# Feed-forward of a decoder layer on one core: silu and product each as one operation over two banks, and the next tile's XT ahead of the product

## What is computed

```python
def _quant_act(x):
    s = jnp.max(jnp.abs(x), axis=-1, keepdims=True) / 127.0 + EPS
    xq = jnp.clip(jnp.round(x / s), -128.0, 127.0)
    return (xq, s)

def _qlinear(x, w):
    wq, ws = _quant_weight(w)
    xq, xs = _quant_act(x)
    y = jnp.einsum('bsi,oi->bso', xq, wq)
    return y * xs * ws
gate = jax.nn.silu(_qlinear(x, w_gate))
up = _qlinear(x, w_up)
return _qlinear(gate * up, w_down)
...
x = _layernorm(x + _L0_ffn_ref(x, L0_ffn_w_gate, L0_ffn_w_up, L0_ffn_w_down), axis=-1)
```

## Time and profile before

| | us |
|---|---|
| median of 3 runs | 390.02 |
| lowest and highest of the 3 | 386.76, 394.39 |
| span of the profiled execution, first to last instruction | 388.1 |

### The profile page before, as it was taken

How to read it: one execution, slowest core, us unless ns; L and a number is a source line. 1 busy time by engine, 2 the same in 40 slices (tenths; PEclk the granted TensorE clock), 3 DMA queues, 4 the chain that set the end, 5 groups by cost and what they waited for, 6 DMA issues and landing times.

```text
span 388.1 us, 9850 instructions
## 1 busy us (share of the span) xinstructions
PE 276.8 (71%) x3140; PEld 176.7 (46%) x3140; DVE 287.3 (74%) x643; ACT 236.9 (61%) x485; POOL 219.2 (56%) x531
## 2 busy tenths in 40 slices
PE   0262652757757258688999999999897666989862
PEld 0131432535545135455566555555564333555441
DVE  4945899997894344477888888888754349999982
ACT  4349254515676033276777677777737428899993
POOL 5301255564687684566888877888501114576773
PEclk9986588869999657699999999999859669999998
DMA  7992000000000131345333435343300000010111
GB/s 198 329 294 47 0 3 0 0 1 0 0 3 0 27 63 28 63 51 77 64 64 65 64 71 83 70 85 66 58 2 3 0 2 0 14 43 27 41 42 54
DMA packets 53042, 20.38 MB, mean 53 GB/s; under 512 B 42256, under 2 KB 52240, under 8 KB 53008
## 3 DMA queue, kind: packets, MB, share of 16 engines
q1 hardware_dynamic: 53008, 19.95, 23.4%
HBM read 9.32 MB, written 2.10 MB: 29 GB/s over the span
## 4 chain that ended last, share of the span: by engine, by line
PE 26%; DVE 13%; POOL 11%; issue 10%; ACT 4%; DMA 2%; SPq 2%; DVEq 1%; POOLq 0%; ACTq 0%
PE psum L1090 7%; DVE M L943 5%; PE psum L1074 4%; PE psum L1048 4%; PE psum L1032 3%; PE psum L1392 3%; PE psum L1124 3%; ACT PB L864 2%; SPq L709 2%; DVE region_q L1367 2%; DMA region_t<-MT 1%; PE psum L1114 1%; DMA kt<-KA 1%; DVE fxabs L1417 1%; DVE KA L919 1%
## 5 line engine op out<-in xcount | busy, mean ns | idle before, releaser
L943 DVE TENSOR_REDUCE M<-psum 128x8 f32<-128x1024 f32 x64 | 77.6, 1213 | 24.4 <-PE psum L1048 24.1
L864 ACT ACTIVATE PB<-psum,exp_scale 128x1024 f32<-128x1024 f32 x64 | 71.6, 1118 | 23.2 <-PE psum L1074 23.1
L1090 PE MATMUL psum<-PB,region_g 128*32 128x128 f32 x1024 | 43.9, 292 | 0.3 <-ACT PB L864 0.3
L1392 PE MATMUL psum<-FW,FXT 128*128 128x512 f16 x128 | 31.2, 388 | 7.5 <-DVE FXT L1372 5.5
L1090 PEld LDWEIGHTS psum<-PB,region_g 128*32 128x32 f32 x1024 | 25.4, 113 | 20.3 <-issue 16.6
L1048 PE MATMUL psum<-kt,region_t 32*128 32x128 f16 x512 | 27.0, 227 | 9.8 <-DVE M L943 7.5
L1074 PE MATMUL psum<-region_t,kt 32*128 32x128 f16 x512 | 26.0, 221 | 4.2 <-ACT PB L864 2.8
L1048 PEld LDWEIGHTS psum<-kt,region_t 32*128 32x128 f16 x512 | 15.4, 97 | 24.2 <-DVE M L943 14.2
L873 ACT ACTIVATE PO<-psum 128x512 f32<-128x512 f32 x16 | 9.6, 597 | 24.8 <-PE psum L1090 24.8
L1335 ACT ACTIVATE region_q<-psum,gs 128x512 f32<-128x512 f32 x32 | 20.5, 681 | 6.2 <-PE psum L1392 6.1
L1367 DVE TENSOR_TENSOR region_q<-region_q,psum 128x512 f32<-128x512 f32 x32 | 20.8, 684 | 2.5 <-PE psum L1392 1.1
(11 more groups left out here) (211 smaller groups left out, 787.4 us busy)
## 6 DMA issues: line engine op xcount, KB each, us to landing
X<-in_x_dram SPq DMA_DIRECT2D x4, 512.0 KB, 6.5
out_dram<-X SPq DMA_DIRECT2D x16, 128.0 KB, 1.7
region_k<-in_L_ffn_w_gate_dram SPq DMA_DIRECT2D x1, 1024.0 KB, 11.3
region_k<-in_L_ffn_w_up_dram SPq DMA_DIRECT2D x1, 1024.0 KB, 9.9
region_k<-in_L_ffn_w_down_dram SPq DMA_DIRECT2D x1, 1024.0 KB, 11.0
CS<-in_ctx_dram SPq DMA_DIRECT2D x16, 64.0 KB, 1.9
region_t<-MT SPq DMA_DIRECT2D x64, 2.0 KB
region_w<-in_L_attn_Wi_dram SPq DMA_DIRECT2D x1, 256.0 KB, 3.8
```

What stands on the lines that cost most here:

```text
L864: act.activation(PB[c % 2][:], ps_P, ACT.Exp, scale=exp_scale[:, 0:1]).then_inc(exp_done, 1)
L943: dve.tensor_reduce(M[:, j:j + 2, n:n + 4], ps_L, AX.X, ALU.max).then_inc(max_done, 1)
L1090: ins = pe.matmul(ps_v[R * g:R * g + R, c], V[(ph - lag) % NB][:, h], PB[c % 2][:, g // 2, 2 * (g % 2) + e], start=(e == 0), stop=(e == 1) ...
L1392: ins = pe.matmul(psx[n], XT[:, c], w[c][:, half(n)], start=(c == 0), stop=(c == DC - 1))
```

## The change

The two halves of the width are joined: gate occupies banks 0 and 1 and up banks 2 and 3; PE runs the four gate matmuls, then the four up matmuls, with one semaphore each; ACT takes one silu over 1024 columns, DVE makes one product over 1024 columns. In DVE's queue XT of the next tile now stands ahead of the product. The gate scale is worked out once.

```diff
--- before.py
+++ after.py
@@ -1256,7 +1256,7 @@
         return ctx.enter_context(nc.semaphore(name))
 
     xabs = sb("fxabs", [P, B]); xs = sb("xs", [P, B]); xinv = sb("fxinv", [P, B])
-    gs = sb("gs", [P, 2, B])
+    gs = sb("gs", [P, B])
     us = sb("us", [P, B])
     U = sb("FU", [P, D], F16); XT = sb("FXT", [P, DC, P], F16)
     SG = region_q[:, 0:I]
@@ -1272,7 +1272,7 @@
 
     scales_done = sem("fscales_done")
     u_done = sem("fu_done"); xT_done = sem("fxT_done"); XT_done = sem("fXT_done")
-    gate_done, up_done, sg_done, hh_done = ([sem(f"{name}_done{n}") for n in range(2)] for name in ("gate", "up", "sg", "hh"))
+    gate_done = sem("gate_done"); up_done = sem("up_done"); sg_done = sem("sg_done"); hh_done = sem("hh_done")
     habs_done = sem("habs_done"); chain = sem("fchain"); hscale_done = sem("hscale_done"); uh_done = sem("uh_done")
     hT_done = sem("fhT_done"); HT_done = sem("HT_done"); y_done = sem("fy_done"); Y_done = sem("fY_done")
     mean_done = sem("fmean3_done"); var_done = sem("fvar_done"); t1_done = sem("ft1_done"); rstd_done = sem("frstd_done")
@@ -1280,8 +1280,8 @@
 
 
     HI = I // 2
-    ps_gate = [psum[:, 0, :], psum[:, 2, :]]
-    ps_up = [psum[:, 1, :], psum[:, 3, :]]
+    ps_gate = psum[:, 0:2, :].rearrange("p b i -> p (b i)")
+    ps_up = psum[:, 2:4, :].rearrange("p b i -> p (b i)")
     ps_x = psum16[:, 4, 0:D].rearrange("p (c t) -> p c t", t=P)
     ps_hT = psum16[:, 5, :].rearrange("p (c t) -> p c t", t=P)
     ps_y = psum[:, 6, 0:D]
@@ -1329,11 +1329,9 @@
     def scalar(act):
         def step(ph, t0_, t1_, t2, t3, t4, t5, t6):
             if t1_ is not None:
-                for n in range(2):
-                    act.wait_ge(gate_done[n], t1_ + 1)
-                    wait(act, hh_done[n], t1_)
-                    act.activation(SG[:, half(n)], ps_gate[n], ACT.Silu,
-                                   scale=gs[:, n, col(t1_)]).then_inc(sg_done[n], 1)
+                act.wait_ge(gate_done, t1_ + 1)
+                wait(act, hh_done, t1_)
+                act.activation(SG[:], ps_gate, ACT.Silu, scale=gs[:, col(t1_)]).then_inc(sg_done, 1)
             if t5 is not None:
                 act.wait_ge(mean_done, t5 + 1)
                 wait(act, var_done, t5)
@@ -1358,21 +1356,19 @@
                 dve.wait_ge(rstd_done, t6 + 1)
                 dve.tensor_scalar(OUT[:, t6, :], Y[:, t6, :], nmean[:, col(t6)], rstd[:, col(t6)], ALU.add,
                                   ALU.mult).then_inc(out_done, 1)
-            if t1_ is not None:
-                hh = HH[:, (ph + 1) % 2]
-                for n in range(2):
-                    dve.wait_ge(sg_done[n], t1_ + 1)
-                    dve.wait_ge(up_done[n], t1_ + 1)
-                    wait(dve, uh_done, t1_ - 1)
-                    dve.tensor_tensor(hh[:, half(n)], SG[:, half(n)], ps_up[n], ALU.mult).then_inc(hh_done[n], 1)
             if t0_ is not None:
                 dve.wait_ge(xT_done, t0_ + 1)
                 if t1_ is not None:
-                    dve.wait_ge(up_done[1], t1_ + 1)
+                    dve.wait_ge(up_done, t1_ + 1)
                 dve.tensor_scalar(XT[:], ps_x, -ROUND, None, ALU.add).then_inc(XT_done, 1)
             if t1_ is not None:
-                for n in range(2):
-                    dve.wait_ge(hh_done[n], t1_ + 1)
+                hh = HH[:, (ph + 1) % 2]
+                dve.wait_ge(sg_done, t1_ + 1)
+                dve.wait_ge(up_done, t1_ + 1)
+                wait(dve, uh_done, t1_ - 1)
+                dve.tensor_tensor(hh, SG[:], ps_up, ALU.mult).then_inc(hh_done, 1)
+            if t1_ is not None:
+                dve.wait_ge(hh_done, t1_ + 1)
                 dve.tensor_reduce(habs[:, col(t1_)], hh, AX.X, ALU.max,
                                   apply_absolute_value=True).then_inc(habs_done, 1)
             if t4 is not None:
@@ -1385,12 +1381,16 @@
         def step(ph, t0_, t1_, t2, t3, t4, t5, t6):
             if t1_ is not None:
                 pe.wait_ge(XT_done, t1_ + 1)
+                wait(pe, sg_done, t1_)
                 for n in range(2):
-                    for psx, w, free, done in ((ps_gate, gateT, sg_done, gate_done), (ps_up, upT, hh_done, up_done)):
-                        wait(pe, free[n], t1_)
-                        for c in range(DC):
-                            ins = pe.matmul(psx[n], XT[:, c], w[c][:, half(n)], start=(c == 0), stop=(c == DC - 1))
-                        ins.then_inc(done[n], 1)
+                    for c in range(DC):
+                        ins = pe.matmul(ps_gate[:, half(n)], XT[:, c], gateT[c][:, half(n)], start=(c == 0), stop=(c == DC - 1))
+                ins.then_inc(gate_done, 1)
+                wait(pe, hh_done, t1_)
+                for n in range(2):
+                    for c in range(DC):
+                        ins = pe.matmul(ps_up[:, half(n)], XT[:, c], upT[c][:, half(n)], start=(c == 0), stop=(c == DC - 1))
+                ins.then_inc(up_done, 1)
             if t3 is not None:
                 pe.wait_ge(uh_done, t3 + 1)
                 wait(pe, HT_done, t3)
@@ -1419,8 +1419,7 @@
         dve.tensor_scalar(xs[:, t], xabs[:, t], 1.0 / QMAX, EPS, ALU.mult, ALU.add).then_inc(scales_done, 1)
         dve.wait_ge(scales_done, 3 * group + 2)
         dve.reciprocal(xinv[:, t], xs[:, t])
-        for n in range(2):
-            dve.tensor_scalar(gs[:, n, t], xs[:, t], wmean[:, GATE:GATE + 1], None, ALU.mult)
+        dve.tensor_scalar(gs[:, t], xs[:, t], wmean[:, GATE:GATE + 1], None, ALU.mult)
         dve.tensor_scalar(us[:, t], xs[:, t], wmean[:, UP:UP + 1], None, ALU.mult).then_inc(scales_done, 1)
         dve.wait_ge(scales_done, 3 * group + 3)
 
```

## The result

The kernel after took 398.66 us (median of four runs) beside 392.2 for before (four runs); ratio 1.0197, 95% interval 1.0122 to 1.0272. Two later comparisons of the same two kernels gave 1.0175 (1.0087 to 1.0263) and 1.0131 (1.0053 to 1.0208). The ratios leave out runs that are over 1.5% above the fastest of their kernel; over all runs of the study, none left out, before has a mean of 393.1 (46 runs, standard error 0.7) and after 397.9 (19 runs, 0.9): +4.8 us with a standard error of 1.1, or 1.2%. All three intervals lie above 1, so the change is slower, by one to two per cent. The forecast was +4.0 us; the median of the first comparison lies above the forecast's own range (392 to 395.3) and inside the whole one (387.5 to 399).

The account below looks back on a forecast made before the run. A ring of waits through DVE, POOL and ACT, 7.55 us per two loop steps, bounds the kernel. Loop +1.65, ramp +2.6, scale -0.2 give +4.0 on 390.0: 394.0 us, own range 392 to 395.3, with rivals 387.5 to 399.

Parts of the forecast that it names:

- Joined silu 1.12, product 1.22, maximum 0.15 behind it: Feed-forward loop: joined silu 1.12 us (pair 1.25), joined product 1.22 (pair 1.28), maximum starting 0.15 after the product.
- The ramp: Unrolled feed-forward steps 1 to 5 before the loop: +0.48 in step 1, +2.1 over steps 2 to 5; +2.6 us.
- XT's trip: Ramp: XT waits for PE's transposes of U, so the maximum comes 2.22 us after U, before 1.73.
- The ring after: Loop: the waits from Y to the Y two steps on take 7.88 us against 7.55; five pairs, +1.65 us.
- Both arrive together: Loop: XT lets the product start at 362.32, the silu ends at 362.31, so XT costs nothing beyond the silu.
- One scale less: Gate scale worked out once: 0.1 us saved, on the path in two of three groups, -0.2 us.
- PE's order: All gate products ahead of all up products on PE, which starts earlier in the ramp; no gain counted.
- fewer operations pay: Rival, chance 0.12: DVE's queue sets the loop's period, so fewer operations save 1.2 to 3.7 us, about 387.6.
- PE's wait: Rival, chance 0.05: PE's 5.5 us of waiting for XT is on the path and all comes back, 384.5.
- the clock: Rival, chance 0.11: TensorE's clock falls to half in the longer ramp; two stretches lose 6.8 us, 400.8.
- the prediction's rule: Clock rival's price: a stretch of 6.8 us at half clock does half its work, so 3.4 us are lost.
- The sum of the edits: Whole kernel: loop 1.65 plus ramp 2.6 less scale 0.2, +4.0 us, time 394.0, +1.0%.

Follow-up runs that it names:

- e6: The kernel before, with POOL's mean moved behind the next step's chain, one pipeline stage later; 393.01 us, ratio 0.9969 (0.989 to 1.0047).
- e1: The kernel after, with XT put back behind the product, silu and product still joined; 395.0 us, ratio 1.0121 (1.0017 to 1.0225).
- e3: The kernel after, with XT behind the product in the written-out steps 1 to 5 only; 394.62 us, ratio 1.0079 (0.9995 to 1.0164).
- e2: The kernel before, halves kept, with XT moved ahead of the two products; 398.96 us, ratio 1.0208 (1.0114 to 1.0303).
- e8: Silu joined alone: the kernel after with XT behind the product and the product in two halves again; 399.92 us, one run.

## Where the prediction was right, and where it failed

- *Joined silu 1.12, product 1.22, maximum 0.15 behind it.* Right: 1.10, 1.215, and 347.94 - 347.79 = 0.15. From the first product to XT behind it is 1.19 in halves (e6, 358.75 to 359.94) and 1.14 joined (e1, 331.30 to 332.44): an operation fewer saves 0.05. The Trainium skill, "VectorE: DVE Perf Modes", section "The TRN2 errata", has the memory's latency exposed between instructions; by its formula, as an estimate, an operation fewer would save 0.157, and here the measurement decides.
- *The ramp.* XT's trip is exposed as forecast (U to the maximum 2.2: 2.18). Steps 2 to 5 are longer by 0.47, 0.44, 0.40 and 0.53 at full clock, +1.84 for the +2.1 predicted. Step 1 with the saved scale, from the first U to the first maximum, is +0.3 (13.68 for 13.37, means of six and three; before's three differ by 0.4) for +0.48 - 0.2. The size is right, but the step that put this loss on XT's place alone failed: with XT back in its old place the ramp gains 0.4 of the 1.8 (e3), since the join alone (e1) makes a ring of 3.73 there.
- *The ring after, 7.88 a pair.* The size was right (7.84 in the pair shown), the releaser was not. "Both arrive together" failed by 0.1: XT comes last in one step of two. In the others DVE has no gap at all and its own row takes 3.8. The loop cost +1.3 instead of +1.65; its pairs are 7.79 on average (38.97 over five), not 7.88.
- *One scale less, PE's order.* As predicted: PE's 5.5 us of waiting for XT went, and no time came of it. The rivals "fewer operations pay" and "PE's wait" are out.
- *The failing step is the clock.* It was a rival with a chance of 0.11, a price of 6.8 us, and no part in the sum. It came in three profiles of six, and its price is 2.7 in FF: 1.1 in the ramp (17.3 for 16.2) and 1.6 in the tail. By the prediction's rule, half of a stretch at half clock, the 10.4 us at half clock would have cost 5.2; work of other engines lies beside the slower matmuls. The whole time from the first U to the last normalisation is 79.8 in before, 83.2 in after at full clock and 86.1 with the falls: +3.4 or +6.3, +4.8 on average over the six. The +4.8 of all runs is the same, though with its standard error of 1.1 it would fit +3.4 or +6.3 too. The sum of the edits (+4.0) was a little high for the full clock (+3.4), and what the profiles have above it is the falls, in half of them. That the change brings these falls is likely by the profiles, and not settled.
- Of the 4.7 us between 398.66 and the forecast's 394.0, 2.2 lie in the base: the median of before was 390.02 then and is 392.2 with the fourth run. The rest of the +6.5 between the two medians of the first comparison is within the spread of four executions: the starts of the feed-forward alone differ by 11 us from one profile to another.

## What to carry to other kernels

An operation that stands between a product and the operation that needs it can fill a gap and be free, as XT was here (1.47 with it and without it); before moving it, ask what will fill the gap, and what round trip the new place exposes. Two halves cost little more than one whole (1.28 for 1.215) and let the next engine start after half (0.68 of silu here, not 1.10): where a ring of waits sets the period, a join puts the second half into that ring, and here joining only one of the two coupled operations cost more than joining both. When steps grow longer with the same PE work, put the clock into the sum with a chance and a price from the stage, not beside it.

## What was not expected

- The parts don't add up: FF is longer by 3.1 with the joins alone (e1), by some 4.2 with the move alone (e2, its fall taken off), by 4.0 with one join (e8), and by 3.1 with everything.
- Taking POOL's mean out of the ring shortens the feed-forward of before by 2.4 us (65.0 to 62.6); the timing (0.9969, 0.989 to 1.0047) is too wide to show 0.6%. It is the best version here by its profile, and only by that.
- The same program had a fall of the clock or none, and with it 2.7 us; the two kinds differ by some tenths of a us in the time of the last rise.
